# Squares of real and imaginary memory summed by an accumulating DMA, with the result's accumulating DMA issued earlier on GpSimd's queue

## The chip, the cores and the metric

One core of a Trainium2 chip runs the whole kernel. The metric is the time of one execution on the device in microseconds (us); lower is better. The core has five engines with an instruction stream each: TensorE (PE, whose weight loads are shown apart as PEld), VectorE (DVE), ScalarE (ACT), GpSimd (POOL) and SyncE (SP), and 16 DMA engines that they share. The streams meet at semaphores only.

## The reference

The input is `x` of 16 sequences x 1024 positions x 256 features, in float32. One layer of a phase mixer is followed by one feed-forward layer. The part that matters here is the mixer, on `x` after a layer norm:

```python
omega = einsum('bsd,ed->bse', x, W_omega) + b_omega
phi = cumsum(omega * exp(log_scale) * pos_scale, axis=1)
cos_phi, sin_phi = cos(phi), sin(phi)
cm_real, cm_imag = x * cos_phi, x * sin_phi
mem_real = cumsum(cm_real, axis=1) / position
mem_imag = cumsum(cm_imag, axis=1) / position
ret_real = mem_real * cos_phi + mem_imag * sin_phi
ret_imag = mem_imag * cos_phi - mem_real * sin_phi
context = concatenate([cm_real, cm_imag, ret_real, ret_imag], axis=-1)
h = _layernorm(context, ln_gamma, ln_beta)
h = gelu(einsum('bsd,ed->bse', h, W1) + b1)
x = x + (x_normed + einsum('bsd,ed->bse', h, W2) + b2)
```

The feed-forward layer then adds `relu(norm(x) @ Wq1 + b1) @ Wq2 + b2`, with weights quantised to -1, 0 and 1. The variance of `context` needs the sum of its squares. Since the squares of sine and cosine add up to one, the squares of `ret_real` and `ret_imag` sum to those of `mem_real` and `mem_imag`; the kernel forms the latter.

## The kernel before

The sequences are cut into 32 chunks of 512 positions. Features lie on the partitions in the mixer, so a chunk's tile is 128 partitions x 1024 float32 (two blocks of 128 features, 512 positions each), which is 512 KB. All matmuls work on float16 pairs of a high and a low part.

The order is written out by hand. Each engine has a function `step` that is run once per chunk and works on several chunks at once: `now` is in the feed-forward layer, `nxt` (one later) in the mixer's two matrix products, `ahead` (two later) in sines, sums and retrieval, `far` (three later) in its first norm. `before` is the chunk that has left. Nothing reorders work: an engine stands at a wait until it is met, and what is behind it on that engine stands too.

The names that matter:

- `sqr`, `turn`: tiles of the chunk `ahead`. ACT writes the squares of the real memory to `sqr` (`square_real`, L652) and of the imaginary memory to `turn` (`square_imag`, L661). `turn` also holds the phase's whole turns (`whole_turns`, L608) and the phase's magnitude (L624).
- `square_sums` (L531 to L537, POOL): adds `turn` to `sqr` (L535, 1024 elements on each partition), then adds the two halves of `sqr` (L537, 512 elements). Ahead of both it waits for `cl_done[3]`, the last low part of the context on DVE (`context_lo`, L1332).
- The sum is rounded by ACT to `q_hi` (`sums_hi`, L656), the first instruction of ACT's next step; base scaling (L581), whole turns (L608), the feed-forward's output (L614) and the sine (L620) stand behind it. DVE's next step begins with `fraction` (L1250), which needs the whole turns.
- DVE ends its step with the residual (`mixer_residual`, L1368), which waits for the second mixer product on PE (L1021), and the phase's scans (`phase_sums`, L1237).
- PE's step: four blocks of the wide product `hidden` (L966), with `context_stats` (L939, L945, of `q_hi` and `q_lo`) after the second; then the feed-forward's first product `ffn_in` (L987) interleaved with its second (L1000), the phase's product `omega` (L926) and the second mixer product (L1021).
- `context_variance` on DVE (L1337 to L1349) waits for PE's statistics; POOL's inverse root (L507) waits for it. Behind it DVE forms the low half of the feed-forward's input (`second_lo`, L1392), and SP then issues four DMA transposes (L438) that put it into `turned2`, for which `ffn_in(0)` waits. SP issues four more (L446) later for the phase's product, then a load of rows (L450) and a store of `x1` (L453).
- POOL's DMAs add while they move: `base_bias` (L490), `x1_bias` (L494), `retrieve` (rr<-qa at L483, ri<-qb at L486) and `output_sum` (L498, from `x1` to the output in HBM). `output_sum` is issued after `retrieve`.

Of the kernel before, what the change touches and what calls it, by code (L numbers as in the profile page):

```python
# [17 lines left out]
ALU = mybir.AluOpType  # L18
# [25 lines left out]
def phase_mixer_layer(nc, x, w_omega, b_omega, log_scale, ln_gamma, ln_beta, w1, b1, w2, b2,  # L44
# [17 lines left out]
    with ctx:  # L62
        def sb(name, shape, dt=F32):
            return ctx.enter_context(nc.sbuf_tensor(name, shape, dt))

        def sem(name):
            return ctx.enter_context(nc.semaphore(name))
# [76 lines left out]
        turn = sb("turn", [P, KD, CH])  # L144
# [13 lines left out]
        sqr = sb("sqr", [P, KD, CH])  # L158
# [109 lines left out]
        sqr_done, sqi_done, q2_done, q_done = sem("sqr_done"), sem("sqi_done"), sem("q2_done"), sem("q_done")  # L268
# [61 lines left out]
        def wait(eng, s, value):  # L330
            if not isinstance(value, int) or value > 0:
                eng.wait_ge(s, value)

        def need(eng, s, c, back=0):

            wait(eng, s, c.counts.value(1, c.more + 1 - back))
# [5 lines left out]
        def need_sum(eng, s, c, back=0):  # L342

            wait(eng, s, c.counts.value(16, 16 * (c.more + 1 - back)))
# [18 lines left out]
        def run(eng, step, first):  # L363

            for s in range(first, CHUNKS):
                step(Step(Counts(eng, s - s % 2), s % 2))
# [36 lines left out]
        def first_chunks(eng):  # L403

            return [Chunk(Counts(eng, 0), more) for more in range(2)]

        def prepared(eng):

            eng.wait_ge(p_lo, len(W1_GROUPS))
            eng.wait_ge(p_scales, 3)  # L410
            eng.wait_ge(p_thr, 1)
            eng.wait_ge(p_tab, 16)
# [53 lines left out]
        @block.gpsimd  # L466
        def _(pool):
            pool.memset(ident[:, :], 0.0).then_inc(p_zero, 1)
            pool.wait_ge(p_zero, 1)
            pool.affine_select(out=ident[:, :], in_=ident[:, :], compare_op=ALU.not_equal, fill=1.0, base=0,  # L470
                               pattern=[[-1, P]], channel_multiplier=1).then_inc(p_ident, 1)
            pool.memset(e_base[:, :], 2.718281828459045).then_inc(p_const, 1)
            pool.memset(minus_half[:, :], -0.5).then_inc(p_const, 1)
            pool.memset(one_half[:, :], 0.5).then_inc(p_const, 1)
            pool.wait_ge(p_const, 3)
            def inverse_std_1(c):
                need(pool, ve1_done, c)
                pool.tensor_tensor(rs1[:, c.b], ve1[:, :], minus_half[:, :], ALU.pow).then_inc(rs1_done, 1)

            def retrieve(c):  # L480
                need(pool, ra_done, c)
                need(pool, qa_done, c)
                pool.dma_start(rr[:, :, :], qa[:, :, :], accum_op=ALU.add).then_inc(rr_done, 16)  # L483
                need(pool, rb_done, c)
                need(pool, qb_done, c)
                pool.dma_start(ri[:, :, :], qb[:, :, :], accum_op=ALU.add).then_inc(ri_done, 16)  # L486

            def base_bias(c):
                need(pool, scaled_done, c)
                pool.dma_start(base[:, c.b], b2_rows, accum_op=ALU.add).then_inc(base_biased[c.b], 16)  # L490

            def x1_bias(c):
                need(pool, xs2_done, c)
                pool.dma_start(x1[:, c.b], f_b2_rows, accum_op=ALU.add).then_inc(x1_biased[c.b], 16)  # L494

            def output_sum(c):
                need(pool, out_done, c)
                pool.dma_start(out_v[c.index], x1[:, c.b], accum_op=ALU.add).then_inc(added[c.b], 16)  # L498

            def inverse_std_2(c):  # L500
                need(pool, ve2_done, c)
                pool.tensor_tensor(rs2[:, :], ve2[:, :], minus_half[:, :], ALU.pow).then_inc(rs2_done, 1)

            def inverse_std_context(c):
                need(pool, cve_done, c)
                need(pool, spread_done, c, 1)
                pool.tensor_tensor(crs[:, :], cve[:, :], minus_half[:, :], ALU.pow).then_inc(crs_done, 1)  # L507

            def step(s):
                before, now, nxt, ahead, far = s.chunk(-1), s.chunk(0), s.chunk(1), s.chunk(2), s.chunk(3)  # L510
                if ahead:
                    base_bias(ahead)
                if now:
                    inverse_std_2(now)
                if nxt:
                    square_lo(nxt, ahead)
                if far:
                    inverse_std_1(far)
                if now:
                    x1_bias(now)  # L520
                if nxt:
                    inverse_std_context(nxt)
                if ahead:
                    product_imag_sin(ahead)
                    retrieve(ahead)
                if before:
                    output_sum(before)
                if ahead:
                    square_sums(ahead)

            def square_sums(c):  # L531
                need(pool, sqr_done, c)
                need(pool, sqi_done, c)
                need(pool, cl_done[3], c)
                pool.tensor_tensor(sqr[:, :, :], sqr[:, :, :], turn[:, :, :], ALU.add).then_inc(q2_done, 1)  # L535
                need(pool, q2_done, c)
                pool.tensor_tensor(sqr[:, 0], sqr[:, 0], sqr[:, 1], ALU.add).then_inc(q_done, 1)  # L537

            def square_lo(c, after):
                if after:  # L540
                    need(pool, frac_done, after)
                need(pool, q_done, c)
                need(pool, qh_done, c)
                pool.tensor_tensor(q_lo, sqr[:, 0], q_hi, ALU.subtract).then_inc(ql_done, 1)

            def product_imag_sin(c):
                need(pool, mi_done, c)
                need(pool, sin_done, c)
                need(pool, sumr_done, c)
                need_sum(pool, rr_done, c, 1)  # L550
                pool.tensor_tensor(qa[:, :, :], mi[:, :, :], sn[:, :, :], ALU.mult).then_inc(qa_done, 1)  # L551

            first, second = first_chunks(pool)
            pool.wait_ge(p_om, 32)
            pool.tensor_tensor(exp_ls[:, :], e_base[:, :], lscale[:, :], ALU.pow).then_inc(p_exp, 1)
            inverse_std_1(first)
            pool.wait_ge(p_root, 1)
            pool.tensor_tensor(mags_all[:, 1:2], mags_all[:, 1:2], one_half[:, :], ALU.pow).then_inc(p_max, 1)
            inverse_std_1(second)
            retrieve(first)  # L560
            square_sums(first)
            pool.wait_ge(p_bias, 32)
            base_bias(first)
            prepared(pool)
            run(pool, step, -1)

        @block.scalar
        def _(act):
# [35 lines left out]

            def whole_turns(c):
                need(act, y_done, c)
                need(act, q2_done, c, 1)
                act.activation(turn[:, :, :], ph[:, :, :], ACT.Identity, bias=rounder[:, 0:1]).then_inc(turn_done, 1)  # L608

            def output(c):  # L610
# [126 lines left out]
            def step(s):  # L737
# [10 lines left out]
                if not now:  # L748
                    whole_turns(ahead)
# [4 lines left out]
                if now and ahead:  # L754
                    whole_turns(ahead)
# [114 lines left out]
            for i, (s, w) in enumerate(((p_fw1, fw1_in), (p_fw2, fw2_in))):  # L870
                act.wait_ge(s, 16)
                if i:
                    act.wait_ge(p_abs, i)
                act.activation(dump, w.rearrange("p m d -> p (m d)"), ACT.Abs,
                               accum_out=abs_sums[:, i:i + 1]).then_inc(p_abs, 1)
            act.wait_ge(p_abs, 2)
            whole_turns(first)
            act.wait_ge(p_scales, 2)
            group_hi(1)
# [809 lines left out]
```

## Time and profile before

| what | value |
|---|---|
| median of 3 runs | 1533.1 us (1530.54 to 1534.26) |
| profiled execution, its own time | 1533.96 us |
| its span in the trace | 1532.2 us |
| PE busy | 1470.5 us, 96% |
| DVE busy | 1438.2 us, 94% |
| ACT busy | 1253.4 us, 82% |
| POOL busy | 616.9 us, 40% |
| mean granted clock of PE | 0.991 |

Busy time is the time in which an engine has an instruction in work. The ends of matmuls are modelled, so a busy PE may still lose time between starts. "Idle before" names the instruction that ended a wait.

### The profile page before, as it was taken

Reading aid. Unit: us, or ns where it says so; the run is one execution under the profiler, and the core shown is the slowest. Engines: PE = TensorE matmul, PEld = TensorE weight load, DVE = VectorE, ACT = ScalarE, POOL = GpSimd, SP = SyncE. Lnnn points to the kernel's source line nnn. Section 1 sums busy time; section 2 is a strip of 40 time slices with the busy share of each in tenths; the row PEclk is TensorE's granted clock in tenths of the full one; section 3 lists DMA queues with packets and bytes.
Section 4 is the critical chain, followed back from the end, with each engine's and each line's share of the span. In section 5 each row is a group of like instructions: output and inputs, shape, how many; then the busy total and the mean of one; then the engine's idle time right before and its main releaser. Section 6 shows DMA issues by size and latency. Waiting matters only on the chain.

```text
span 1532.2 us, 29929 instructions
## 1 busy us (share of the span) xinstructions
PE 1470.5 (96%) x10685; PEld 878.0 (57%) x10685; DVE 1438.2 (94%) x2325; ACT 1253.4 (82%) x1773; POOL 616.9 (40%) x393
## 2 busy tenths in 40 slices
PE   3779999999999999999999999999999999999998
PEld 2445566656555665555665655566565566555556
DVE  7999999999999999999999999999999999989954
ACT  6768888888988888988888898888888788888756
POOL 1333444433354443444444334444344444334331
PEclk9899999999999999999999999999999999999999
DMA  6325545555645655654555564455565455555452
GB/s 219 67 58 111 102 80 109 108 111 113 123 76 100 111 104 111 124 107 79 105 111 110 111 125 94 83 111 103 109 125 109 73 109 111 110 111 101 73 90 42
DMA packets 231427, 158.20 MB, mean 103 GB/s; under 512 B 138608, under 2 KB 221552, under 8 KB 231280
## 3 DMA queue, kind: packets, MB, share of 16 engines
q0 software_dynamic: 59376, 83.37, 34.3%
q1 hardware_dynamic: 170272, 69.25, 18.4%
q10 hardware_dynamic: 1632, 3.67, 0.7%
q8 instruction: 86, 1.41, 0.4%
q14 instruction: 61, 0.50, 0.1%
HBM read 24.13 MB, written 33.03 MB: 37 GB/s over the span
## 4 chain that ended last, share of the span: by engine, by line
DVE 35%; PE 24%; issue 14%; ACT 12%; POOL 7%; DMA 4%; SPq 2%; DVEq 1%; ACTq 0%; POOLq 0%
PE ps L966 11%; DVE arena L1332 5%; POOL sqr L535 4%; DVE arena L1400 4%; PE ps L1000 4%; PE ps L987 4%; POOL sqr L537 3%; PE ps L1021 3%; ACT xs L601 3%; DVE mr L1285 3%; ACT base L581 3%; DVE arena L1361 2%; DVE bn L1170 2%; DVE arena L1356 2%; DVE qb L1316 2%
## 5 line engine op out<-in xcount | busy, mean ns | idle before, releaser
L966 PE MATMUL ps<-arena,w_hi 128*128 128x512 f16 x2048 | 609.2, 379 | 3.0 <-DVE arena L1332 1.6
L966 PE MATMUL ps<-arena,w_lo 128*128 128x512 f16 x1024 | 388.3, 379 | 0.0
L966 PEld LDWEIGHTS ps<-arena,w_hi 128*128 128x128 f16 x2048 | 197.5, 98 | 224.2 <-issue 2.0
L987 PE MATMUL ps<-turned,fw_t 128*128 128x512 f16 x1024 | 250.6, 380 | 8.6 <-DMA turned<-rows 4.1
L1000 PE MATMUL ps<-fw_t,arena 128*128 128x256 f16 x2048 | 255.0, 273 | 1.9 <-DVE arena L1400 1.9
L1000 PEld LDWEIGHTS ps<-fw_t,arena 128*128 128x128 f16 x2048 | 197.8, 97 | 63.8 <-issue 16.7
L704 ACT ACTIVATE arena<-ps,relu_bias,relu_scale 128x512 f32<-128x512 f32 x256 | 197.0, 769 | 24.8 <-PE ps L987 24.4
L535 POOL TENSOR_TENSOR sqr<-sqr,turn 128x1024 f32<-128x1024 f32 x32 | 84.3, 2635 | 323.3 <-DVE arena L1332 323.3
L1400 DVE TENSOR_TENSOR arena<-arena 128x512 f16<-128x512 f32 x256 | 172.0, 681 | 19.5 <-ACT arena L713 17.5
L1021 PE MATMUL ps<-w_hi,arena 128*128 128x256 f16 x1024 | 172.9, 273 | 0.3 <-issue 0.3
L966 PEld LDWEIGHTS ps<-arena,w_lo 128*128 128x128 f16 x1024 | 100.0, 98 | 121.0
L987 PEld LDWEIGHTS ps<-turned,fw_t 128*128 128x128 f16 x1024 | 97.5, 98 | 109.4 <-DVE arena L1356 14.6
L713 ACT CAST arena<-arena 128x512 f16<-128x512 f32 x256 | 154.5, 615 | 4.3
L1021 PE MATMUL ps<-w_lo,arena 128*128 128x256 f16 x512 | 139.6, 273 | 0.0
L656 ACT CAST sqr<-sqr 128x512 f16<-128x512 f32 x32 | 19.8, 617 | 128.4 <-POOL sqr L537 128.4
L483 POOL DMA_DIRECT2D rr<-qa x32 | 29.5, 921 | 203.4 <-DVE rr L1322 203.4
L551 POOL TENSOR_TENSOR qa<-mi,sn 128x1024 f32<-128x1024 f32 x31 | 73.3, 2364 | 86.5 <-DVE mr L1285 86.5
L1021 PEld LDWEIGHTS ps<-w_hi,arena 128*128 128x128 f16 x1024 | 100.0, 98 | 12.6 <-issue 0.7
L670 ACT ACTIVATE arena<-arena,b_full,z_down 128x512 f32<-128x512 f32 x128 | 96.9, 804 | 10.9 <-DVE arena L1356 10.8
L1361 DVE SCALAR_TENSOR_TENSOR arena<-arena,up 128x512 f16<-128x512 f32 x128 | 92.0, 741 | 0.0
L1356 DVE TENSOR_TENSOR arena<-ps,rb 128x512 f32<-128x512 f32 x128 | 82.0, 682 | 8.9 <-ACT rb L666 6.2
L676 ACT ACTIVATE arena<-arena,up 128x512 f16<-128x512 f32 x128 | 88.1, 713 | 1.0
(189 smaller groups left out, 2850.4 us busy)
## 6 DMA issues: line engine op xcount, KB each, us to landing
x_rows<-in_L_attn_x SPq DMA_DIRECT2D x32, 512.0 KB, 6.5
rr<-qa POOLq DMA_DIRECT2D x32, 512.0 KB, 6.2
ri<-qb POOLq DMA_DIRECT2D x32, 512.0 KB, 9.0
base<-bias_rows POOLq DMA_DIRECT2D x32, 512.0 KB, 5.5
x<-bias_rows POOLq DMA_DIRECT2D x32, 512.0 KB, 5.5
out<-x SPq DMA_DIRECT2D x31, 512.0 KB, 7.6
out<-x POOLq DMA_DIRECT2D x31, 512.0 KB, 11.2
arena<-in_L_attn_W ACTq DMA_DIRECT2D x1, 2048.0 KB, 11.8
```

Of the source, the lines that this page charges most:

```text
L535: pool.tensor_tensor(sqr[:, :, :], sqr[:, :, :], turn[:, :, :], ALU.add).then_inc(q2_done, 1)
L670: act.activation(z[:, m], z[:, m], ACT.Gelu, scale=z_down[:, 0:1], bias=b1_full[:, m:m + 1])\
L676: act.activation(gh[:, m], z[:, m], ACT.Copy, scale=up[:, 3:4]).then_inc(gh_done[m], 1)
L704: act.activation(rf[:, m % SLOTS], ps[:, 4 + m % KE], ACT.Relu, scale=relu_scale[:, 0:1], bias=relu_bias[:, m:m + 1]).then_inc(relu_done, 1)
L713: act.copy(rh[:, m % SLOTS], rf[:, m % SLOTS]).then_inc(rh_done, 1)
L966: last = pe.matmul(ps[:, 4 + m], w[:, k, m * P:(m + 1) * P], a[:, c.b, k], start=(i == 0), stop=(i == len(passes) - 1))
L987: last = pe.matmul(ps[:, 4 + m % KE], fw1_t[:, k, m * P:(m + 1) * P], a[:, k], start=(i == 0), stop=(i == len(passes) - 1))
L1000: last = pe.matmul(ps_rows_a[:, j], a[:, m % SLOTS, j * P:(j + 1) * P], fw2_t[:, m], start=(m == 0 and j % 2 == 0 and a is rh), stop=(m == ...
L1021: last = pe.matmul(rows[:, j], a[:, m, j * P:(j + 1) * P], w[:, m], start=(i == 0), stop=(i == len(passes) - 1))
L1356: dve.tensor_tensor(z[:, m], ps[:, 4 + m], rb[:, :], ALU.mult).then_inc(z_done[m], 1)
L1361: dve.scalar_tensor_tensor(out=gl[:, m], in0=z[:, m], scalar=up[:, 3:4], in1=gh[:, m], op0=ALU.mult, op1=ALU.subtract).then_inc(gl_done[m], 1)
L1400: dve.tensor_tensor(rl[:, m % SLOTS], rf[:, m % SLOTS], rh[:, m % SLOTS], ALU.subtract)\
```

## The change

The whole-tile sum on POOL becomes a DMA of 512 KB that adds `turn` to `sqr`. It is issued once both squares are there, and no longer waits for `cl_done[3]`; POOL then waits for its landing and for `cl_done[3]` before it adds the halves. `output_sum` moves ahead of POOL's product (L551, `product_imag_sin`) and of both retrieval DMAs. ACT's wait in `whole_turns` counts the semaphore in the DMA's steps of 16.

```diff
                     inverse_std_context(nxt)
+                if before:
+                    output_sum(before)
                 if ahead:
                     product_imag_sin(ahead)
                     retrieve(ahead)
-                if before:
-                    output_sum(before)
                 if ahead:
                     square_sums(ahead)
 
             def square_sums(c):
                 need(pool, sqr_done, c)
                 need(pool, sqi_done, c)
+                pool.dma_start(sqr[:, :, :], turn[:, :, :], accum_op=ALU.add).then_inc(q2_done, 16)
+                need_sum(pool, q2_done, c)
                 need(pool, cl_done[3], c)
-                pool.tensor_tensor(sqr[:, :, :], sqr[:, :, :], turn[:, :, :], ALU.add).then_inc(q2_done, 1)
-                need(pool, q2_done, c)
                 pool.tensor_tensor(sqr[:, 0], sqr[:, 0], sqr[:, 1], ALU.add).then_inc(q_done, 1)
...
             def whole_turns(c):
                 need(act, y_done, c)
-                need(act, q2_done, c, 1)
+                need_sum(act, q2_done, c, 1)
```

## Rows read from the trace of the kernel before

**Rows 1.** Timeline of POOL, 604 to 638 us: start, length, line, idle before.

```profile
604.28 2.83 POOL L535 TENSOR_TENSOR sqr<-sqr,turn 128x1024 f32<-128x1024 f32 x1 [10.61 <-DVE arena L1332]
607.19 2.07 POOL L537 TENSOR_TENSOR sqr<-sqr 128x512 f32<-128x512 f32 x1
...
622.05 1.93 POOL L507 TENSOR_TENSOR crs<-cve,minus_half 128x4 f32<-128x4 f32 x1 [1.91 <-DVE cve L1349]
626.83 2.36 POOL L551 TENSOR_TENSOR qa<-mi,sn 128x1024 f32<-128x1024 f32 x1 [2.85 <-DVE mr L1285]
```

**Rows 2.** Timeline of ACT, from 609 us.

```profile
609.29 0.62 ACT L656 CAST sqr<-sqr 128x512 f16<-128x512 f32 x1 [3.60 <-POOL sqr L537]
...
611.79 1.13 ACT L608 ACTIVATE turn<-ph,rounder 128x1024 f32<-128x1024 f32 x1
...
640.91 1.05 ACT L661 ACTIVATE turn<-mi 128x1024 f32<-128x1024 f32 x1
```

**Rows 3.** Timeline of DVE, at 63 us and from 602 us.

```profile
63.30 4.40 DVE L1237 TENSOR_TENSOR_SCAN ph<-ones,ph_carry,ph 128x512 f32<-128x512 f32 x2
...
602.88 1.22 DVE L1332 TENSOR_TENSOR arena<-ri,arena 128x1024 f16<-128x1024 f32 x1 [0.45 <-ACT arena L633]
...
604.82 1.28 DVE L1368 SCALAR_TENSOR_TENSOR x<-ps,h_down,base 128x1024 f32<-128x1024 f32 x1
606.01 4.33 DVE L1237 TENSOR_TENSOR_SCAN ph<-ones,ph_carry,ph 128x512 f32<-128x512 f32 x2
...
612.96 1.23 DVE L1250 SCALAR_TENSOR_TENSOR ph<-turn,ph 128x1024 f32<-128x1024 f32 x1 [0.64 <-ACT turn L608]
...
617.50 2.46 DVE L1271 TENSOR_TENSOR_SCAN mi<-ones,mi_carry,cmi 128x512 f32<-128x512 f32 x2
...
621.21 0.16 DVE L1337 TENSOR_SCALAR cmu<-ps 128x4 f32<-128x4 f32 x1
```

**Rows 4.** Timeline of PE, 603 to 634 us.

```profile
603.87 0.27 PE L1021 MATMUL ps<-w_hi,arena 128*128 128x256 f16 x1
...
618.56 0.34 PE L945 MATMUL ps<-ones_h,sqr 128*128 128x1 f16 x8
...
629.70 2.75 PE L987 MATMUL ps<-turned,fw_t 128*128 128x512 f16 x12
```

**Rows 5.** Timeline of POOL: the sum at L535 in four chunks, L537 in one.

```profile
107.52 2.34 POOL L535 TENSOR_TENSOR sqr<-sqr,turn 128x1024 f32<-128x1024 f32 x1 [10.12 <-DVE arena L1332]
109.93 1.27 POOL L537 TENSOR_TENSOR sqr<-sqr 128x512 f32<-128x512 f32 x1
...
829.36 2.64 POOL L535 TENSOR_TENSOR sqr<-sqr,turn 128x1024 f32<-128x1024 f32 x1 [10.07 <-DVE arena L1332]
874.33 2.64 POOL L535 TENSOR_TENSOR sqr<-sqr,turn 128x1024 f32<-128x1024 f32 x1 [10.07 <-DVE arena L1332]
...
1375.71 2.63 POOL L535 TENSOR_TENSOR sqr<-sqr,turn 128x1024 f32<-128x1024 f32 x1 [12.82 <-DVE arena L1332]
```

**Rows 6.** The list of waits: who waited, for whom, total us, times, longest.

```profile
PEld ps L987 <- DVE arena L1356: 14.6, 23, 1.2
...
PEld ps L987 <- DMA turned<-rows: 8.4, 10, 1.5
...
PEld ps L926 <- DMA turned<-xs: 3.5, 1, 3.5
```

**Rows 7.** Timeline of SP, the transposes in mid-run and in the tail.

```profile
623.18 5.12 SPq L438 DMA_TRANSPOSE turned<-rows  x4
...
1477.21 7.46 SPq L438 DMA_TRANSPOSE turned<-rows  x4
```

**Rows 8.** Answer for line L438, window 1476 to 1478 us, and for the whole run.

```profile
DMA to landing us min/median/max: 6.0/6.0/6.0
...
DMA to landing us min/median/max: 2.4/2.5/6.0
```

**Rows 9.** Timeline of POOL, the biases' and output's DMAs issued at 1475 and 1515 us.

```profile
1475.10 1.33 POOL L494 DMA_DIRECT2D x<-bias_rows  x1 [2.51 <-ACT xs L601]
...
1514.93 1.30 POOL L498 DMA_DIRECT2D out<-x  x1 [4.37 <-ACT x L614]
```

**Rows 10.** DMA traffic: GB/s in 40 slices, of 1476 to 1486, and of 1514.9 to 1526 us.

```profile
GB/s 0 0 0 4 139 168 180 168 172 184 168 160 168 180 180 143 90 136 247 235 211 182 55 7 0 8 8 10 7 68 209 209 39 0 38 139 144 200 97 144
...
GB/s 0 0 0 0 0 0 7 70 74 85 159 181 177 199 185 203 199 199 111 33 7 0 0 0 0 0 0 0 0 0 0 0 0 0 0 0 0 30 0 0
```

**Rows 11.** The profile's DMA issues: each 512 KB, median us to landing.

```profile
rr<-qa POOLq DMA_DIRECT2D x32, 512.0 KB, 6.2
ri<-qb POOLq DMA_DIRECT2D x32, 512.0 KB, 9.0
...
out<-x POOLq DMA_DIRECT2D x31, 512.0 KB, 11.2
```

## The prediction

> **What bounds the kernel now.** I read the table of busy times first: PE is busy for 1470.5 us of a span of 1532.2 us, DVE for 1438.2. Whatever the change frees on other engines, only the time in which PE does not start matmuls can be won. The timeline of POOL at one fixed point of every chunk then gives the period: from the sum at 107.52 to that at 1375.71 us lie 28 chunks of 45.29 us each; a common period without a visible DMA stall is 44.97 [rows 5]. The list of waits says what PE lacks inside these periods. Its weight loads stood before `ffn_in` 23 times for DVE's scaled hidden block (L1356), 14.6 us, 10 times for the transposes of rows, 8.4 us, and once for the other transposes, 3.5 us [rows 6]. About 0.12 us of each is no loss, because loads that follow one another directly have such a gap too (a matmul every 0.216 us, a load of 0.098). That leaves 11.8, 7.2 and 3.4 us, 22.4 in all, or 0.8 us for each of the 28 chunks, of which a part is caught up within the chunk. So the period without stalls is between 45.29 - 0.80 = 44.5 and 44.8; I take 44.65. The most that the middle of the run can give is 28 x 0.64 = 18 us, 1.2%. POOL's 7% on the chain of waits (4% L535, 3% L537 in the profile's part 4) is not the gain: take it away and PE's own work is next, 0.64 us behind.
>
> **Why DVE is late.** In the chunk at 600 us, POOL starts its sum at 604.28, right after the last context part on DVE (602.88 + 1.22), and ends both additions at 609.26 [rows 1, 3]. Two things hang on it. ACT stands 3.60 us for the halves' sum and only then scales, rounds the turns (ends 612.92) and lets DVE's fraction start at 612.96, after an idle 0.64 [rows 2, 3]. And DVE's two phase scans, which run at the same time as POOL's additions, take 4.33 us, while two scans of the same size with no POOL addition beside them (L1271) take 2.46 [rows 3]. The difference, 1.87 us, is time in which DVE and POOL hold each other up: the shorter addition takes 2.07 us here.
>
> **The change, part by part.**
>
> *The sum L535 goes.* Its 2.83 us (2.6 in most chunks) leave POOL and the chain. The halves' sum is left. It may start when DVE's last context part is done (604.1) and may be held up to 0.7 us by a relu's low part on DVE; without a scan beside it I give it 1.3 us (it took 1.27 at 109.93 [rows 5]), so it ends at about 606.1 in place of 609.26. DVE's residual cannot move much: it waits for PE's last L1021, which ends at 604.14 [rows 4], so it starts 0.65 us earlier at best and the scans at 605.4. They lose some 0.6 us to the halves' sum and end at 608.5 in place of 610.34; the fraction starts at about 610.5 in place of 612.96. DVE gains 2.45 us of lead. What follows on DVE stays in order until `context_variance`, which needs PE's statistics: done at 618.90, taken up at 621.21 [rows 3, 4]. So the lead is capped at 2.3 us. That covers the late hidden block (0.75 us of idle PE in this chunk, 1.24 us the longest of its loads): the 11.8 us of rows 6 go.
>
> *The DMA sqr<-turn comes.* It is issued when ACT has squared the imaginary memory, at 641.96 [rows 2], and by then both retrieval DMAs are out. No row shows it; the nearest are rr<-qa with 6.2 us and ri<-qb with 9.0 us [rows 11], both adding in SBUF at the same size. It is needed by DVE's last context part, at 604.1 + 45.3 = 649.4, that is 7.4 us after its issue. I take 6.5 us, because the output's DMA no longer runs beside it. Up to 7.4 it costs nothing. At 9.0 the halves' sum slips 1.6 us into the scans and eats about that much of the 2.3 us of lead. POOL pays some 0.9 us to issue it, at a time when it waited 10.61 us [rows 1]. Behind POOL's new wait stand only the halves' sum and the next step's `base_bias`, which waited for ACT anyway.
>
> *The output's DMA moves ahead.* POOL has nothing to do between the inverse root (ends 623.98) and the product at 626.83 [rows 1]; the issue's 1.3 to 1.65 us fit there, and its semaphore (ACT's output, some 10 us older) is long up. The queue costs nothing. The traffic does. SP's four transposes of `ffn_in`'s input go out from 623.18 [rows 7], call it T0; each lands 2.5 us after its issue [rows 8], the last at T0 + 3.84 + 2.5 = T0 + 6.3 = 629.5, and PE starts `ffn_in` at 629.70 [rows 4]. There is no slack there now. The output's DMA was issued 14 us later, beside the retrieval. Now it is issued at T0 + 0.8, whatever the lead is, because the inverse root and the transposes both follow `context_variance`. Alone, such a DMA moves its bytes from about 2.2 us after its issue for 3.2 us [rows 9, 10]: from T0 + 3.0 to T0 + 6.2, over the third and the fourth transpose. The tail shows one such meeting. There the bias' DMA, issued at 1475.10, moves at its usual rate from 1477 to 1479.75 as if alone, and the transposes issued from 1477.21 get the engines afterwards [rows 7, 9, 10]. The first lands after 6.0 us in place of 2.5 [rows 8], SP needs 7.46 us for the four in place of 5.12 [rows 7], and the last is some 3 us late. Here only two of four are hit. From below: they follow directly on the output's bytes and land at T0 + 8.0, 1.7 us late. From above: the third fares as the tail's first (T0 + 2.56 + 6.0 = 8.56) and the fourth 0.5 us behind it, at T0 + 9.1, 2.8 us late. Against it stands the lead: T0 moves 2.3 us earlier against PE, so PE wants the data at T0 + 8.6 or 8.7. The loss is 0 to 0.5 us a chunk, with the stray late landings that already cost 7.2 us on top. I take 0.35 us, toward the tail's row since it is the only meeting seen.
>
> **The Trainium skill's rule on this.** "DMA: Bandwidth & Descriptors", the section on queues, rings and completion order, says that each DMA engine takes turns between the queue rows it has work for, packet by packet. By it the transposes would get half of each engine beside the output's bytes. The trace does not agree in the tail, where the first queue kept its full 168 to 184 GB/s. By the rule the loss would be nought and the time that of the first rival.
>
> **Sum.** Against the profiled execution's 1533.96 us (1.8 us around the span): hidden block -11.8, transposes 28 x 0.35 = +9.8, the one 3.4 us stall for the phase's transposes gone because SP issues these earlier while rr<-qa (bound to PE's relu) does not -3.4, start of the run (the first scans' 4.40 us [rows 3] become less than 3) -1.5. That is -6.9: 1527.1. The median of the runs lies 0.9 below the profiled execution, so 1526.
>
> **Rivals.**
>
> *The transposes are not held.* Engines shared fairly, or the last landing within T0 + 8.6: then no 9.8 is paid, and the lead also absorbs part of the stray landings. 1533.1 - 18 - 1.5 = 1513.6, or up to 1517 if a part of the stray ones stays. For it: two transposes have their bytes through before the output's begin. Against: the tail. Chance 0.25.
>
> *The transposes outrun the lead: slower.* The place is PE before `ffn_in(0)`. The mechanism is the one above; the price is 28 times what the last landing exceeds the lead's 8.6 us. Break-even is where it eats the savings, (11.8 + 3.4 + 1.5) / 28 = 0.6 us, a last landing at T0 + 9.2 with full lead. If the squares' DMA takes 9 us, the lead is 1.5 us and the upper bound of 9.1 gives 1.3 us a chunk: 28 x 1.3 - 16.7 = +20, 1553. With 1.0 us it is 1544. Against: the period's other slack. Chance 0.22.
>
> *It cancels.* The squares' DMA is late by some us or the output's DMA costs 0.5 to 0.75 us: 1530 to 1536. For it: both engines near their limit. Chance 0.18.
>
> **How the numbers follow.** The forecast itself has 0.35, with 1520 to 1531 (0.15 to 0.5 us a chunk). A difference under 0.3%, 4.6 us, can't be told from none. Faster: 0.27 of the 0.35, and 0.25: 0.52. Same: 0.08 and 0.18: 0.26. Slower: 0.22. The range reaches from 1514 (no loss at the transposes) to 1546 (1.0 us a chunk); beyond it I leave about 2 in 10.
>
> **What would show it.** L535 gone, L537 near 1.3 us and starting just after DVE's last context part; the scans L1237 at 1.3 to 1.6 us each in place of 2.2; ACT's wait before L656 down by 2 to 3 us; squares' DMA landing in 6 to 7 us; waits of L987 for L1356 gone; landings of L438 up to 4 to 6 us for two in four, with waits of L987 for turned<-rows in most chunks in place of 10. The prediction is wrong upward if those waits exceed 0.6 us a chunk, and downward if the landings stay at 2.5 us.

## The result, and the profile after

The changed kernel takes 1537.51 us, the kernel before, run beside it, 1532.23 us (medians of 11 runs each). One run of the changed kernel took 2216 us at a mean granted clock of 0.723, and the ratio leaves it out. The ratio is 1.0034, with a 95% interval of 1.002 to 1.0047: slower by a third of a percent, where 1526 us was forecast. The time lies inside the range given, the sign is wrong. The profiled execution has a span of 1535.9 us, 3.7 more than before.

Everything that the change was to free has been freed. The timelines of POOL, DVE and PE of the changed kernel, in a chunk in which PE's statistics stand where they stood in [rows 4] (618.58 against 618.56 us), so that times compare directly with [rows 1 to 4]:

```profile
603.82 1.58 POOL L537 TENSOR_TENSOR sqr<-sqr 128x512 f32<-128x512 f32 x1 [5.53 <-DVE arena L1332]
...
619.81 1.94 POOL L507 TENSOR_TENSOR crs<-cve,minus_half 128x4 f32<-128x4 f32 x1 [2.89 <-DVE cve L1349]
621.71 1.28 POOL L498 DMA_DIRECT2D out<-x  x1
```

```profile
605.40 2.45 DVE L1237 TENSOR_TENSOR_SCAN ph<-ones,ph_carry,ph 128x512 f32<-128x512 f32 x2
...
609.74 1.22 DVE L1250 SCALAR_TENSOR_TENSOR ph<-turn,ph 128x1024 f32<-128x1024 f32 x1
...
618.96 0.16 DVE L1337 TENSOR_SCALAR cmu<-ps 128x4 f32<-128x4 f32 x1 [0.89 <-PE ps L945]
```

```profile
618.58 0.34 PE L945 MATMUL ps<-ones_h,sqr 128*128 128x1 f16 x8
...
629.58 3.62 PE L987 MATMUL ps<-turned,fw_t 128*128 128x512 f16 x16
```

The scans take 2.45 us in place of 4.33, the fraction starts 3.2 us earlier against PE, and DVE now stands 0.89 us for PE's statistics, which before it took up 2.3 us late in this chunk and 1.6 us late in the median one. DVE's busy time falls from 1438.2 to 1370.9 us. The DMA of the squares lands after a median 5.2 us and is hardly waited for (4 times in 32 chunks, 19.5 us of POOL's time).

PE waits for something else. The list of waits of the changed kernel, and below it two lines of the kernel before that [rows 6] does not have (PE's own waits; [rows 6] has those of its weight loads):

```profile
PEld ps L987 <- DMA turned<-rows: 27.3, 26, 2.2
DVE cmu L1337 <- PE ps L945: 27.3, 30, 4.6
PE ps L987 <- DMA turned<-rows: 15.3, 17, 1.7
```

```profile
PE ps L987 <- DMA turned<-rows: 4.1, 7, 1.0
PE ps L987 <- DVE arena L1356: 3.6, 10, 0.7
```

No wait of PE for L1356 is left, and its waits for the transposes of rows have grown from 4.1 to 15.3 us. What closes the loop is told by the chain of waits, here in one of the chunks with a long stall (start, length, what):

```profile
800.76 0.21 PE ps L945 x8
...
801.67 1.24 DVE rows L1392
...
802.98 1.20 SPq L438
...
805.52 2.85 SPq L438
...
808.41 4.79 DMA turned<-rows
...
813.25 3.63 PE ps L987 x16
```

From PE's statistics over DVE's variance and low half, SP's four transposes and their landing it is 12.3 us back to PE. The way itself takes 2.0 us to the first issue; the transposes take 10.3, where in [rows 7, 8] they took 6.3. SP's third issue stands 2.85 us, and the fourth transpose lands 4.79 us after its issue.

The periods say what that costs. These are PE's statistics in the second chunk and 28 chunks later, of the changed kernel and of the kernel before:

```profile
119.42 1.74 PE L939 MATMUL ps<-ones_h,arena 128*128 128x1 f16 x64
...
1393.21 1.74 PE L939 MATMUL ps<-ones_h,arena 128*128 128x1 f16 x64
```

```profile
120.67 1.49 PE L939 MATMUL ps<-ones_h,arena 128*128 128x1 f16 x54
...
1390.86 1.29 PE L939 MATMUL ps<-ones_h,arena 128*128 128x1 f16 x46
```

The period is 45.49 us against 45.36. The best experiment below runs all of these chunks but one in 44.85 or 44.86, and no run goes below 44.84 there: I take it as PE's floor. So over 28 periods the kernel before lost 14.4 us and the changed one loses 18.0: +3.6. The start is 1.25 us shorter (119.42 against 120.67), what follows the last of these rows 1.35 us longer (1535.9 - 1393.21 against 1532.2 - 1390.86). The sum is +3.7 us, the difference of the spans. The longer end lies in the last two periods (90.20 us against 88.85, from 1393.21 to 1483.41 and from 1390.86 to 1479.71), in the second of which PE waits 1.1 us for the transposes of rows again.

### The profile page after: what moved, and what is told of

It reads as the page before. It is cut to its first block, busy times and chain, and to the rows that moved or that the text cites. A ratio compares the mean times of both kernels' runs of the same rounds, so it can differ in the third digit from the quotient of the medians.

```text
span 1535.9 us, 29961 instructions
## 1 busy us (share of the span) xinstructions
PE 1472.3 (96%) x10685; PEld 878.3 (57%) x10685; DVE 1370.9 (89%) x2325; ACT 1254.3 (82%) x1773; POOL 554.6 (36%) x393
## 4 chain that ended last, share of the span: by engine, by line
PE 79%; SPq 7%; DMA 6%; DVE 5%; issue 1%; ACT 1%; ACTq 0%; POOL 0%; DVEq 0%
PE ps L966 30%; PE ps L1000 14%; PE ps L987 14%; PE ps L1021 11%; SPq L438 7%; PE ps L926 5%; DMA turned<-rows 5%; PE ps L939 3%; DVE rows L1392 2%; DMA arena<-in_L_attn_ln_beta 1%; PE ps L945 0%; PE ps L952 0%; DVE arena L1332 0%; DVE qb L1316 0%; DVE cvar L1345 0%
## 5 line engine op out<-in xcount | busy, mean ns | idle before, releaser
L987 PE MATMUL ps<-turned,fw_t 128*128 128x512 f16 x1024 | 247.4, 379 | 15.9 <-DMA turned<-rows 15.3
L537 POOL TENSOR_TENSOR sqr<-sqr 128x512 f32<-128x512 f32 x32 | 49.1, 1535 | 173.3 <-DVE arena L1332 153.8
L1356 DVE TENSOR_TENSOR arena<-ps,rb 128x512 f32<-128x512 f32 x128 | 82.3, 685 | 29.6 <-ACT rb L666 25.7
L507 POOL TENSOR_TENSOR crs<-cve,minus_half 128x4 f32<-128x4 f32 x32 | 60.2, 1880 | 91.8 <-DVE cve L1349 91.8
L551 POOL TENSOR_TENSOR qa<-mi,sn 128x1024 f32<-128x1024 f32 x31 | 72.9, 2350 | 50.3 <-DVE mr L1285 50.3
```

The costliest lines, as they stand in the source:

```text
L987: last = pe.matmul(ps[:, 4 + m % KE], fw1_t[:, k, m * P:(m + 1) * P], a[:, k], start=(i == 0), stop=(i == len(passes) - 1))
L1356: dve.tensor_tensor(z[:, m], ps[:, 4 + m], rb[:, :], ALU.mult).then_inc(z_done[m], 1)
```

## The experiments

Times are medians; each is compared with the kernel before on the same chip (1531.7 to 1533.7 us there).

**The squares by DMA alone.** The output's DMA goes back behind the retrieval.

```diff
-                if before:
-                    output_sum(before)
                 if ahead:
                     product_imag_sin(ahead)
                     retrieve(ahead)
+                if before:
+                    output_sum(before)
```

> The squares are added by DMA, the output's DMA stays behind the retrieval as before. My theory (the whole loss is the output's traffic meeting the transposes of ffn_in's input, and the squares' DMA itself gains DVE its lead): waits of L987 for the transposes fall from 27 us to under 8, those for L1356 stay near 0, period 44.9, time 1518 to 1524, ratio about 0.993. Rival (the squares' DMA queued behind the output's lands late, 9 us or more after its issue, and DVE's scans are held by the halves' sum again): 1528 to 1535, ratio 0.998 to 1.002, with a wait of L537 for the DMA above 60 us.

Measured: 1525.93 us, ratio 0.9961 (0.9939 to 0.9984), between the two forecasts. The wait for the squares' DMA is the rival's (230.7 us in 30 waits of L537; it lands after 8.6 us, behind the output's), but it spoils the scans in some chunks only: in 20 of 32 one of the two takes over 2 us, and the median of all is 1.27. The waits of the weight loads for L1356 fall from 14.6 to 3.2 us. That is 11.4 us of load gaps, and the 28 periods became 7.1 us shorter (45.36 to 45.11), of which 5.1 are one stall that this run does not have, the one for the phase's transposes in [rows 6] (a single period of 49.98 us). The load gaps were worth a fraction of their length.

**The output's DMA early alone.** The squares stay on POOL.

```diff
+                if before:
+                    output_sum(before)
                 if ahead:
                     product_imag_sin(ahead)
                     retrieve(ahead)
-                if before:
-                    output_sum(before)
```

> The output's DMA goes early, the squares are added on POOL as before. My theory: the transposes land about as late as in the changed kernel, but without DVE's lead of 2.3 us they start later against PE; PE stalls 2 to 3 us a chunk for them, and the time is 1575 to 1610, ratio 1.03 to 1.05. Rival (the place of the output's DMA costs little, the loss came from the added 512 KB of DMA): 1528 to 1540, ratio within 0.997 to 1.005.

Measured: 1593.22 us, ratio 1.0391 (1.036 to 1.0422), as the theory had it. PE's waits for the transposes:

```profile
PE ps L987 <- DMA turned<-rows: 57.7, 28, 3.2
```

The landings (median 4.7, longest 8.2 us) are those of the changed kernel (4.7 and 8.1). The squares' DMA, and with it DVE's lead, is all that separates 1593 from 1537.5.

Not all of the price is waiting. The 28 periods are 69 us over the floor, the waits 57.7. Seven times, after a wait of 2.1 to 2.6 us, PE then ran for some 4 us at 1.2 GHz, the lower of its two levels. The clock missing in these stretches adds up to the other 12 us; the changed kernel has no such stretch in mid-run. One of the seven, by the answer for windows of 2 us (window; length, PE busy, instructions; granted clock; DMA share, GB/s):

```profile
984.00:986.00 2.00, 0.50 (x3) 1.00 0.51 93
986.00:988.00 2.00, 2.00 (x7) 0.57 0.62 126
```

**The output's DMA ten microseconds earlier.** Squares by DMA.

```diff
                 if now:
                     inverse_std_2(now)
+                if before:
+                    output_sum(before)
                 if nxt:
                     square_lo(nxt, ahead)
...
-                if before:
-                    output_sum(before)
                 if ahead:
                     product_imag_sin(ahead)
```

> Squares by DMA, the output's DMA issued right after inverse_std_2, some 10 us ahead of where the changed kernel has it and before the biases' second DMA. My theory: its bytes are through before the transposes of rows start; their landings are back near 2.5 us, period 44.85 to 44.95, time 1516 to 1521, ratio 0.992. Rival (it delays square_lo, x1_bias or the statistics by its 1.3 us on POOL, or pushes the bias' DMA into the transposes): waits of L987 for transposes over 15 us, 1528 or more, ratio 0.998 or more.

Measured: 1518.48 us, ratio 0.9901 (0.9869 to 0.9933), the theory's time. No wait of PE itself for the transposes of rows or for L1356 is left in the list. PE's statistics in the same two chunks as above:

```profile
120.01 1.74 PE L939 MATMUL ps<-ones_h,arena 128*128 128x1 f16 x64
...
1376.22 1.74 PE L939 MATMUL ps<-ones_h,arena 128*128 128x1 f16 x64
```

That is 44.865 us a chunk. Of the kernels that compute the whole result it is the fastest.

**The output's DMA between the product and the retrieval.** Squares by DMA.

```diff
+                if ahead:
+                    product_imag_sin(ahead)
                 if before:
                     output_sum(before)
                 if ahead:
-                    product_imag_sin(ahead)
                     retrieve(ahead)
```

> Squares by DMA, the output's DMA issued between POOL's product and the retrieval, about T0 + 6. My theory: its bytes move at T0 + 8 to T0 + 11, behind the transposes of rows and over those for the phase's product, for which PE has some 2 to 3 us in hand; waits of L987 for transposes under 8 us, some waits of L926; time 1518 to 1525, ratio 0.992 to 0.996. Rival (any transfer beside any transposes costs alike): as the changed kernel, 1535 to 1540, ratio 1.003.

Measured: 1522.21 us, ratio 0.9929 (0.9905 to 0.9954), as the theory had it. Its bytes now meet the transposes for the phase's product, whose median landing rises from 2.5 to 3.6 us. Nearly all periods are at 44.85 us still; the profiled execution has two stalls for these transposes, in periods of 47.8 and 49.3 us; behind the second, PE is at the lower clock for 4 us.

**Half of the output's DMA, at the changed kernel's place.** The residual is not added to the other half of the output.

```diff
-pool.dma_start(out_v[c.index], x1[:, c.b], accum_op=ALU.add)
+pool.dma_start(out_v[c.index][:, 0:2], x1[:, c.b, 0:2], accum_op=ALU.add)
```

> The changed kernel, but the output's early DMA carries only the first two of the four row blocks, 256 KB in place of 512 (the residual is not added to the other half of the output). Everything else, its issue on POOL included, stays. Theory (it is the time that the output's bytes hold the engines over the transposes): they hold them 1.6 us less, the last of the four transposes lands inside DVE's lead, waits of PE's L987 for the transposes fall from 15.3 us to under 3, period 44.85 to 44.95, time 1518 to 1523. Rival (a fixed cost of a DMA from POOL beside transposes, whatever its size, or POOL's issue): waits stay over 10 us, 1533 or more. Between them the cost would be proportional to the bytes: waits near 7 us, about 1527.

Measured: 1518.47 us, ratio 0.9901 (0.9882 to 0.992). PE does not wait for the transposes, the period is 44.86. The same number of DMAs at the same place costs nothing at half the bytes, so neither the DMA as such nor its issue is the price. Whether it is the bytes or the number of packets that carry them, no run tells, since both were halved.

**Three quarters of it.** As above with three of the four row blocks (`0:3`).

> The changed kernel with three of the four row blocks in the output's early DMA, 384 KB (the residual is not added to the last block of the output). With 256 KB the period was 44.86, with 512 KB 45.49. If the transposes are late in proportion to the bytes and DVE's lead absorbs a fixed part, 0.8 us less lateness than with 512 KB leaves a stall only where a stray landing adds to it: period 44.86 to 45.1, waits of PE's L987 for transposes 1 to 6 us, time 1519 to 1526. Rival (cost proportional to the bytes from 256 KB on): period 45.2, 1528.

Measured: 1522.69 us, ratio 0.9935 (0.9919 to 0.9951). PE's waits for the transposes are 3.2 us, the period 45.02. With 256, 384 and 512 KB the loss over the floor is 0.01, 0.17 and 0.64 us a chunk: a threshold, then a rise, as when a fixed lead is used up.

**The output's DMA ten microseconds earlier, squares on POOL.**

```diff
                 if now:
                     inverse_std_2(now)
+                if before:
+                    output_sum(before)
                 if nxt:
                     square_lo(nxt, ahead)
```

(with the old `output_sum` behind the retrieval taken out)

> Squares added on POOL as in the kernel before, the output's DMA issued after inverse_std_2, as in the best kernel so far (1518.5). The difference to that kernel is what the squares' DMA alone is worth (DVE's lead); the difference to the kernel before is what the output's place behind the retrieval costs. Reading one (what PE itself waits, 3.6 us for L1356, is the loss; loads' gaps are not): this kernel keeps DVE late, periods 44.85 to 45.3 as before, 1527 to 1533, waits of PE's L987 for L1356 of 2 to 6 us. Reading two (the loads' gaps of 14.6 us are the loss): the same time here, but then the squares' DMA must be worth 12 us or more, so 1531 to 1535. Rival to both (the retrieval DMAs' delay by the output's bytes was the true limit and the squares' sum never mattered): 1519 to 1523.

Measured: 1563.87 us, ratio 1.02 (1.0177 to 1.0222). All three forecasts missed. The place had a cost that I had not seen, on POOL and DVE:

```profile
626.54 1.32 POOL L498 DMA_DIRECT2D out<-x  x1
627.38 1.67 POOL L544 TENSOR_TENSOR sqr<-sqr 128x512 f16<-128x512 f32 x1
```

```profile
627.51 1.58 DVE L1180 TENSOR_SCALAR ve<-mv 128x4 f32<-128x4 f32 x1
```

The DMA's issue pushes `square_lo` onto DVE's L1180, four columns that took 0.23 us in the kernel before and now take 1.58, and so in 29 of 32 chunks. DVE had no lead to lose: 1.35 us of delay made the period 1.0 us longer (46.37). The best kernel has the same meeting (L1180 takes 1.57 us there, in 29 of 32 chunks) and pays nothing: there DVE takes up PE's statistics 0.4 us late in the median chunk, here 2.85. So this run does not price the squares' DMA by itself, but it shows what a late DVE costs.

**The output's DMA after the product, squares on POOL.** To price the squares' DMA without that meeting.

```diff
                 if ahead:
                     product_imag_sin(ahead)
-                    retrieve(ahead)
                 if before:
                     output_sum(before)
+                if ahead:
+                    retrieve(ahead)
```

> Squares on POOL as before, the output's DMA between POOL's product and the retrieval. Beside the kernel with the same place and the squares by DMA (1522.2) it prices the squares' DMA alone, without the meeting of a POOL addition and a small DVE instruction that spoiled the earlier try. Reading one (DVE's lateness costs what PE itself waits for L1356, 3.6 us, and takes away the cover for late transposes and stray landings): 1529 to 1536, 7 to 14 us more than 1522. Reading two (the place of the output's DMA is all, the squares do not matter): 1519 to 1525.

Measured: 1595.52 us, ratio 1.0428 (1.0398 to 1.0458), 73 us over the same place with the squares by DMA; again far outside both forecasts. PE waits for the other transposes (L927 here is L926 of the kernel before):

```profile
PE ps L927 <- DMA turned<-xs: 45.6, 14, 5.4
DVE xf L1221 <- DMA turned<-xs: 27.4, 11, 4.1
```

I had taken this place as harmless, because it is harmless with the lead. It is not without it. As in the run with the output's DMA early alone, part of the price is clock: eight stretches at the lower level between 120 and 1450 us, behind waits of 3.2 to 5.4 us, cost about 17 us. The four pairs, in us:

| place of the output's DMA | squares on POOL | squares by DMA |
|---|---|---|
| behind the retrieval (kernel before) | 1532.6 | 1525.9 |
| after the context's inverse root (the change) | 1593.2 | 1537.5 |
| after the product | 1595.5 | 1522.2 |
| after `inverse_std_2` | 1563.9 | 1518.5 |

**The transposes untied from the statistics.** The changed kernel, two calls swapped on DVE.

```diff
-                if nxt:
-                    context_variance(nxt)
                 if now:
                     second_lo(now)
+                if nxt:
+                    context_variance(nxt)
```

> The changed kernel with two calls swapped on DVE: the low half of the feed-forward's input (second_lo, L1392) ahead of the context's variance. The output's DMA keeps its place and its full 512 KB. Theory: in the changed kernel the transposes are tied to PE's statistics by DVE's order, and the output's DMA follows the same statistics 0.8 us behind them. Untied, the transposes go out some 1.2 to 1.7 us earlier against PE and the output's DMA 0.2 us later, so the last landing is within the time that PE needs anyway: waits of PE's L987 for the transposes from 15.3 us to under 5, period 44.85 to 45.0, time 1518 to 1523. Rival (the transposes are starved by the output's bytes wherever they stand, and the lead plays no part): 1533 or more with over 10 us of these waits.

Measured: 1526.91 us, ratio 0.9955 (0.9934 to 0.9975). PE's waits for the transposes fall from 15.3 to 6.5 us, the period to 45.18: between the two forecasts. The end of the chain in a stalled chunk, from SP's third issue on:

```profile
803.10 1.27 SPq L438
...
804.41 6.86 DMA turned<-rows
```

The tie was real: in the median chunk the transposes go out 0.5 us behind PE's statistics in place of 2.0, and that wins 10.6 us. But the last one lands 6.86 us after its issue. Its end, 811.3, is 8.2 us behind the issue of the output's DMA (803.10); in the changed kernel it was 9.4 (813.2 against 803.76) and in a mild chunk 7.8 (629.5 against 621.71). In each of the 29 chunks in mid-run, of either kernel, the last transpose landed after the output's DMA had landed. The third did so in all 29 of the changed kernel, but in only 12 here. So going out earlier saves the third in most chunks and the fourth in none.

## Why the prediction was wrong, step by step

*What bounds the kernel* was right: PE has about half a microsecond a chunk to give. The floor I took was too low, 44.65 us; it is 44.85, so 14.4 us were to be had in the 28 periods, not 18.

*Why DVE is late* and *the sum goes* were right, and too modest: the scans fell to 2.45 us and the fraction moved 3.2 us, where 2.45 was forecast. The cap by PE's statistics was right, with 0.89 us to spare.

*The DMA of the squares* was right: 5.2 us to landing, where I took 6.5. Alone it gains 6.7 us.

*The output's DMA moves ahead* had the right mechanism, and its place (PE before `ffn_in(0)`) was named there and in the slower rival. Its working was off. I gave the last landing T0 + 8.0 to T0 + 9.1; in eleven successive chunks between 530 and 990 us of the changed kernel it came 8.4 to 10.2 us after SP's first issue, 9.3 on average. I had two of the four transposes hit; three are. The second, issued at T0 + 1.24 in the chunk at 803 us and due at T0 + 3.7, landed at T0 + 9.4, as the answer for L438 in the window 804.3 to 805.4 shows:

```profile
DMA to landing us min/median/max: 8.1/8.1/8.1
```

The third landed there at T0 + 9.7, where my upper bound had T0 + 8.56, and the fourth 0.5 us behind it, as I had put it. Yet the term came out near its size, which is luck in part: 0.35 us a chunk more than before were forecast, and PE's own waits for these transposes grew by 15.3 - 4.1 = 11.2 us, 0.40 a chunk. The 0.64 us over the floor hold the stray landings too, which I had counted apart.

*The sum* failed at its largest term, "hidden block -11.8". I took it from gaps between weight loads (14.6 us less 0.12 each). PE's own waits for the same instructions are 3.6 us, so this term was over three times too large. Weight loads run ahead of the matmuls, so a gap of half a microsecond between loads can cost PE a tenth. The timelines of PE and of its weight loads in the kernel before show it:

```profile
842.61 1.74 PE L939 MATMUL ps<-ones_h,arena 128*128 128x1 f16 x64
...
887.56 1.74 PE L939 MATMUL ps<-ones_h,arena 128*128 128x1 f16 x64
```

```profile
858.05 0.55 PEld L987 LDWEIGHTS ps<-turned,fw_t 128*128 128x128 f16 x4 [0.58 <-DVE arena L1356]
```

The period around this gap of 0.58 us is 44.95, 0.10 over the floor. The run with the squares' DMA alone says the same by experiment.

The term for the phase's transposes was too small. That wait of PE is 3.0 us long, but its period is 5.1 us over the floor, because PE then ran at the lower clock: four matmuls take 1.89 us there and 1.03 at full clock.

```profile
1364.21 1.89 PE L926 MATMUL ps<-turned,wo_hi 128*128 128x512 f16 x4 [2.96 <-DMA turned<-xs]
...
1364.00:1366.00 2.00, 1.79 (x5) 0.50 1.03 284
```

The sum, term by term, in us:

| term | forecast | measured |
|---|---|---|
| hidden block | -11.8 | -3.6 (PE's own waits) |
| transposes of rows | +9.8 | +11.2 (PE's own waits) |
| the one stall for the phase's transposes | -3.4 | -5.1 (its period over the floor) |
| start | -1.5 | -1.25 |
| sum | -6.9 | +1.25, of +3.7 between the spans |

The remaining 2.4 us lie in none of these waits and are not placed. The hidden block's 8.2 us are most of the miss of 10.6 and decide the sign: with -3.6 there and every other term as forecast the sum is +1.3.

*The rivals.* The slower one, 0.22, named what happened, but not its size (1544 to 1553) nor quite its reason: its break-even of 0.6 us a chunk rested on savings of 16.7 us. They were 10, which puts it at 0.36, and the transposes took 0.40 more than before. The first rival, and with it the rule of the Trainium skill ("DMA: Bandwidth & Descriptors", the section on queues, rings and completion order) that the engines take turns between queues packet by packet, does not describe the last transposes: one that carries 0.13 MB and lands alone in 2.5 us took 6.86. The DMA queues of the changed kernel show both sides of it, from 806.75 to 808 and from 808 to 809.25 us (packets, MB, share of 16 engines; q0 has POOL's DMAs, q1 SP's):

```profile
q0 software_dynamic: 101, 0.10, 82.5%
q1 hardware_dynamic: 121, 0.03, 33.2%
...
q0 software_dynamic: 244, 0.25, 124.5%
```

In the first stretch the packets are about even in number, as the rule has it, but the output's are four times as large, so that the transposes don't get the half of each engine that I had put down. In the second no packet of SP's queue moves at all, though the second and third transposes are out and have not landed. Where the turns are lost, in the engines or in what feeds them, no run here tells.

What stays open is why the stall differs so much from chunk to chunk (0 to 1.7 us of PE's wait). A late transpose by a microsecond or so appears every third chunk in the kernel before too, and I did not find its cause.

## What to carry to other kernels

When a transfer is moved, look for what is in flight at its new place, and price it by how far the last of those landings moves against the slack of the engine that waits. A lead bought by one half of a change may be what pays for the other half: try the halves apart, and try other places for the moved one, since here the same change with the transfer 10 us earlier is 1% faster in place of 0.3% slower. For PE, count its own waits as loss, not the gaps between its weight loads, and behind a wait of some microseconds look at the granted clock: the period can be longer by more than the wait.

## What the runs showed of the hardware that I had not expected

A DVE instruction of four columns (L1180) took 1.57 us in place of 0.23 when it met a POOL subtraction of 512 columns (L544). In the best kernel the POOL instruction runs from 609.09 to 610.75 and L1180 from 609.21 to 610.78: it was held to the other's end. The Trainium skill says of the port pair that VectorE and GpSimd share ("SBUF — State Buffer", the section on its two separate sides) that it is held for a whole instruction and the other engine blocks; this agrees.

PE's granted clock fell to its lower level for 3.5 to 7.5 us in 18 stretches in mid-run, in five of the eleven kernels, each time behind a wait of PE of 2.1 to 5.4 us. Not every such wait was followed by one: those of 2.8 us in one kernel and 3.2 in another were not.

Of four DMA transposes that met an adding DMA of 512 KB from POOL, the last always landed after it: 7.6 to 10.1 us after that DMA's issue in 29 chunks of the changed kernel, 6.7 to 8.9 in the run with the low half first, where they go out 1.5 us earlier. At half the size none of this reached PE.
